# Three V buffers, outer taps ahead of quantise1, a last step and a seam in a new order, and filler matmuls on TensorE

## What is computed

```python
x = x + tanh(g_xattn) * xattn(layernorm(x), ctx, ctx, Wq, Wk, Wv, Wo)   # 16 heads of 16
x = x + tanh(g_ffn)   * ffn(layernorm(x), w1, conv_w, conv_b, w2)
# ffn: h = bit_linear(x, w1)               256 -> 1024
#      h = silu(depthwise_conv1d(h))       3 taps along the tokens of a sequence
#      y = bit_linear(h, w2)               1024 -> 256
# bit_linear: activations rounded to 255 levels by the absolute maximum of their token,
#             weights rounded to -1, 0, 1 by the mean of |w|
```

## Time and profile before

| | |
|---|---|
| median of three runs | 258.53 us (256.13 to 259.03) |
| the profiled execution | 256.48 us, span 253.8 us |
| TensorE matmul busy | 216.5 us (85%) |
| VectorE busy | 189.2 us (75%) |
| ScalarE busy | 162.6 us (64%) |
| POOL busy | 124.8 us (49%) |
| mean granted TensorE clock | 0.959 of 2.4 GHz |

### The profile page before, as it was taken

How to read it: one execution, slowest core, us unless ns; L and a number is a source line. 1 busy time by engine, 2 the same in 40 slices (tenths; PEclk the granted TensorE clock), 3 DMA queues, 4 the chain that set the end, 5 groups by cost and what they waited for, 6 DMA issues and landing times.

```text
span 253.8 us, 6484 instructions
## 1 busy us (share of the span) xinstructions
PE 216.5 (85%) x2384; PEld 175.8 (69%) x2396; DVE 189.2 (75%) x383; ACT 162.6 (64%) x318; POOL 124.8 (49%) x229
## 2 busy tenths in 40 slices
PE   7898989989899899998999989797943799995964
PEld 7786777877768677776777768565633588884853
DVE  3354567879779878888878888777599599996741
ACT  2568785567758787877878768464742477763531
POOL 3320353473455767567675675635367223444440
PEclk9999999999999999999999999978696899998899
DMA  6961011011011010100000000000000011101111
GB/s 177 381 211 41 16 32 43 4 44 41 3 41 33 15 43 3 41 3 21 4 4 0 3 4 0 3 0 3 0 0 0 0 46 41 44 24 42 41 42 62
DMA packets 9489, 9.86 MB, mean 39 GB/s; under 512 B 1011, under 2 KB 9203, under 8 KB 9459
## 3 DMA queue, kind: packets, MB, share of 16 engines
q1 hardware_dynamic: 9458, 9.46, 11.6%
HBM read 7.36 MB, written 2.10 MB: 37 GB/s over the span
## 4 chain that ended last, share of the span: by engine, by line
POOL 31%; issue 23%; DVE 22%; PE 19%; ACT 3%; DMA 1%; POOLq 0%; SPq 0%; DVEq 0%; ACTq 0%
POOL rstd L324 5%; DVE zmax L1088 5%; POOL hid L348 4%; POOL xn L334 4%; DVE y L993 3%; PE ps_av L676 3%; DVE y L996 3%; POOL xn L328 3%; POOL xn L316 3%; POOL rstd L308 3%; POOL var L321 3%; DVE qa L973 3%; PE ps_score L603 2%; PE ps_score L452 2%; DVE xres L1098 2%
## 5 line engine op out<-in xcount | busy, mean ns | idle before, releaser
L937 DVE TENSOR_REDUCE smax<-ps_max 128x8 f32<-128x1024 f32 x31 | 37.9, 1223 | 20.5 <-PE ps_max L462 16.9
L749 ACT ACTIVATE prob<-ps_score 128x1024 f32<-128x1024 f32 x32 | 32.7, 1023 | 18.2 <-PE ps_score L452 17.2
L452 PE MATMUL ps_score<-Qs,KT 32*128 32x128 f32 x512 | 37.8, 286 | 3.5 <-ACT QT L744 1.7
L452 PEld LDWEIGHTS ps_score<-Qs,KT 32*128 32x128 f32 x512 | 32.0, 189 | 11.2 <-issue 10.1
L462 PE MATMUL ps_max<-KT,QT 32*128 32x256 f32 x248 | 35.1, 400 | 0.0
L357 POOL TENSOR_SCALAR zq<-y,zmax 128x1024 f16<-128x1024 f32 x16 | 18.3, 1143 | 30.9 <-issue 14.9
L321 POOL TENSOR_SCALAR var<-mv 128x1 f32<-128x1 f32 x16 | 7.9, 496 | 43.2 <-DVE mv L969 43.1
L423 PE MATMUL ps_proj<-xnT,wq 128*128 128x128 f32 x128 | 18.4, 287 | 6.2 <-ACT xnT L723 6.0
L423 PEld LDWEIGHTS ps_proj<-xnT,wq 128*128 128x128 f32 x128 | 15.6, 191 | 9.1 <-ACT xnT L723 8.7
L462 PEld LDWEIGHTS ps_max<-KT,QT 32*128 32x128 f32 x248 | 21.1, 184 | 0.1
L1088 DVE TENSOR_REDUCE zmax<-y 128x1 f32<-128x1024 f32 x16 | 19.4, 1214 | 2.3 <-ACT y L882 2.3
(11 more groups left out here) (138 smaller groups left out, 537.8 us busy)
## 6 DMA issues: line engine op xcount, KB each, us to landing
cin<-ctxT SPq DMA_DIRECT2D x16, 128.0 KB, 2.1
xres<-x SPq DMA_DIRECT2D x16, 128.0 KB, 2.5
out<-xres SPq DMA_DIRECT2D x16, 128.0 KB, 1.7
w1f<-w1T SPq DMA_DIRECT2D x1, 1024.0 KB, 5.6
w2f<-w2T SPq DMA_DIRECT2D x1, 1024.0 KB, 7.9
wk<-wkT SPq DMA_DIRECT2D x1, 256.0 KB, 2.8
wv<-wvT SPq DMA_DIRECT2D x1, 256.0 KB, 3.9
wq<-wqT SPq DMA_DIRECT2D x1, 256.0 KB, 4.2
```

Source lines behind the costliest of these rows:

```text
L452: mm = pe.matmul(ps_score[:, i * 512 + j * P:i * 512 + (j + 1) * P], KT[b % 3][rows, j * P:(j + 1) * P], Qs[rows, j * P:(j + 1) * P], star ...
L749: act.activation(prob[pair][:, :], ps_score[:, :], ACT.Exp, scale=DH ** -0.5).then_inc(exp_done, 1)
L937: dve.tensor_reduce(dst, first_max(n, pair)[:, :].rearrange("p (g t e k) -> p g t e k", g=PG, t=KD, e=2), AX.X, ALU.max).then_inc(max_done, 1)
```

## The change

V gets a third buffer, so `v_copy(n)` waits for `weigh(n-3)`. In `step` on VectorE the odd tile's outer taps stand ahead of `quantise1`. Step 15 becomes a function `last_step` of its own on three engines, with another order; POOL does its tile before `round1` there. The weight work is spread: a half of a weight sum in each of steps 1 to 4, w1's mean in step 2 and w2's in step 4, w1r's halves in steps 5 and 6. The seam is in a new order on TensorE, ScalarE and VectorE. `y_transpose(12)` and `(13)` move from v = 8 to v = 9, the later two by one as well. `keep_busy` is also put into step 14 and the seam: 4, 3, 2, 3, 12 and 2 matmuls.

```diff
+VB = 3
...
-OPENED.update({LAST - 4: [LAST, LAST + 1], LAST - 3: [LAST + 2], LAST - 2: [LAST + 3]})
+OPENED.update({LAST - 3: [LAST, LAST + 1], LAST - 2: [LAST + 2], LAST - 1: [LAST + 3]})
...
-        V = [sb(f"V{i}", [P, NH * ROW]) for i in range(2)]
+        V = [sb(f"V{i}", [P, NH * ROW]) for i in range(VB)]
...
                 if seq(s - 2):
                     norm2(s - 2)
-                    round1(s - 2)
+                    if s < NB - 1:
+                        round1(s - 2)
                 for T in TILES.get(s, ()):
                     if on_gp(T):
                         dequantise(T)
+                if s == NB - 1:
+                    round1(s - 2)
                 if seq(s + 2):
...
+            def keep_busy(count, bank):
+
+                for i in range(count):
+                    pe.matmul(bank[:, 0:P], ident[:, :], ident[:, :], start=True, stop=True)
...
-                                       V[a % 2][:, h * ROW:(h + 1) * ROW],
+                                       V[a % VB][:, h * ROW:(h + 1) * ROW],
...
                 if seq(n + 1):
                     project_k(n + 1)
-                if s == NB - 1:
-                    y_transpose(0)
+                else:
+                    pe.wait_ge(v_done, NB)
+                    keep_busy(4, ps_k)
+                row_stage(b, 1)
+
+            def last_step():
+                b, a, d = NB - 1, NB - 2, NB - 3
+                T, U_ = TILES[b]
+                project_out(d)
+                hidden(T, LAST)
+                weigh(a)
+                max_transpose(b)
+                int_transpose(d - 1, T)
+                unweighted_transpose(a)
+                row_stage(b, 0)
+                y_transpose(0)
+                hidden(U_, LAST)
+                att_transpose(a)
                 row_stage(b, 1)
...
-            def weight_means():
+            def weight_mean(i):
                 pe.wait_ge(gate_done, 1)
-                pe.wait_ge(abs_done, 1)
+                pe.wait_ge(abs_done[i], 2)
+                if i == 1:
+                    pe.wait_ge(xq_done, 2 * 2)
                 for half in range(2):
-                    mm = pe.matmul(ps_setup[:, 2:4], ones[:, :], abs_sum[:, 2 * half:2 * half + 2],
+                    mm = pe.matmul(ps_setup[:, 2 + i:3 + i], ones[:, :], abs_sum[:, 2 * half + i:2 * half + i + 1],
                                    start=(half == 0), stop=(half == 1))
                 mm.then_inc(sums_ready, 1)
-            step(2, weight_means)
+            step(2, lambda: weight_mean(0))
             pe.wait_ge(mean_done, 1)
             pe.wait_ge(ident16_done, 1)
-            for s in range(3, SB + 2):
+            step(3)
+            step(4, lambda: weight_mean(1))
+            pe.wait_ge(mean_done, 2)
+            step(5)
+            pe.wait_ge(w1q_done, PIECES)
+            for s in range(SB + 2, NB - 1):
                 step(s)
-            pe.wait_ge(w1q_done, PIECES)
-            for s in range(SB + 2, NB):
-                step(s)
+            last_step()
...
             project_out(NB - 2)
             int_transpose(NB - 3, 20)
             weigh(NB - 1)
-            hidden(20, NB - 2)
+            hidden(20, LAST)
             y_transpose(1)
             unweighted_transpose(NB - 1)
-            hidden(21, NB - 2)
+            y_transpose(2)
+            hidden(21, LAST)
+            pe.wait_ge(x1_done, NB - 1)
+            keep_busy(3, ps_xT)
             att_transpose(NB - 1)
-            y_transpose(2)
+            pe.wait_ge(att_done, NB)
+            keep_busy(2, ps_av)
             project_out(NB - 1)
-            hidden(22, NB - 2)
+            keep_busy(3, ps_av)
+            hidden(22, LAST)
+            y_transpose(3)
             int_transpose(NB - 2, 23)
+            keep_busy(12, ps_av)
+            hidden(23, LAST)
             zq_transpose(0)
-            y_transpose(3)
-            hidden(23, NB - 2)
+            keep_busy(2, ps_av)
+            project_down(0)
             int_transpose(NB - 1, 24)
             for v in range(NB):
-                project_down(v)
+                if v > 0:
+                    project_down(v)
                 if v + 1 < NB:
                     zq_transpose(v + 1)
...
-                wait(act, av_ready, NG * (n - 1))
-                act.activation(V[n % 2][:, :].rearrange("p (h w) -> p h w", w=ROW)[:, :, 0:DH],
+                wait(act, av_ready, NG * (n - VB + 1))
+                act.activation(V[n % VB][:, :].rearrange("p (h w) -> p h w", w=ROW)[:, :, 0:DH],
...
                 if seq(a):
                     exponent(a, 1)
-                extra(0)
+                extra()
                 for T in last:
                     middle_tap(T)
...
                 if seq(d - 1):
                     int_copy(d - 1)
-                extra(1)
                 if seq(n):
                     q_copy(n)
...
-                if s == NB - 1:
-                    middle_tap(18)
+            def last_step():
+                b, a, d = NB - 1, NB - 2, NB - 3
+                before, now = TILES[b - 1], TILES[b]
+                exponent(a, 1)
+                middle_tap(before[0])
+                raw_copy(now[0])
+                u_copy(a)
+                middle_tap(before[1])
+                int_copy(d - 1)
+                exponent(b, 0)
+                middle_tap(now[0])
+                att_copy(a)
+                exponent(b, 1)
...
-            def weight_sums(i):
+            def weight_sum(i, k):
                 w, loaded_w = ((w1f, w1_in), (w2f, w2_in))[i]
 
-                def half(k):
+                def half():
                     act.wait_ge(loaded_w, 16)
-                    ac = act.activation(y[:, (2 * i + k) * HID:(2 * i + k + 1) * HID], w[:, k * HID:(k + 1) * HID], ACT.Abs,
-                                        accum_out=abs_sum[:, 2 * k + i:2 * k + i + 1])
-                    if i == 1 and k == 1:
-                        ac.then_inc(abs_done, 1)
+                    act.activation(y[:, (2 * i + k) * HID:(2 * i + k + 1) * HID], w[:, k * HID:(k + 1) * HID], ACT.Abs,
+                                   accum_out=abs_sum[:, 2 * k + i:2 * k + i + 1]).then_inc(abs_done[i], 1)
                 return half
 
-            step(1, weight_sums(0))
+            def first_weights(k):
+                def half():
+                    act.wait_ge(w1q_done, PIECES)
+                    act.activation(w1r[:, k * HID:(k + 1) * HID], w1q[:, k * HID:(k + 1) * HID],
+                                   ACT.Copy).then_inc(w1r_done, 1)
+                return half
+
+            step(1, weight_sum(0, 0))
             act.wait_ge(gate_ready, 1)
             act.activation(gate[:, :], ps_setup[:, 0:2], ACT.Tanh).then_inc(gate_done, 1)
-            step(2, weight_sums(1))
+            step(2, weight_sum(0, 1))
             act.wait_ge(mean_done, 1)
-
-            def first_weights(k):
-                act.wait_ge(w1q_done, PIECES)
-                act.activation(w1r[:, k * HID:(k + 1) * HID], w1q[:, k * HID:(k + 1) * HID], ACT.Copy).then_inc(w1r_done, 1)
-
-            for s in range(3, SB + 1):
+            step(3, weight_sum(1, 0))
+            step(4, weight_sum(1, 1))
+            step(5, first_weights(0))
+            act.wait_ge(small_in, 16)
+            step(6, first_weights(1))
+            for s in range(SB + 3, NB - 1):
                 step(s)
-            step(SB + 1, first_weights)
-            act.wait_ge(small_in, 16)
-            for s in range(SB + 2, NB):
-                step(s)
+            last_step()
...
-            exponent(NB - 1, 1)
-            middle_tap(19)
 
             act.activation(scratch[:, :], ones[:, 0:1], ACT.Silu)
             act.wait_ge(w2q_done, PIECES)
-            act.wait_ge(w1q_done, PIECES)
             u_copy(NB - 1)
             silu(0)
+            middle_tap(19)
             int_copy(NB - 3)
+            silu(1)
             middle_tap(20)
             att_copy(NB - 1)
-            silu(1)
+            silu(2)
             middle_tap(21)
-            silu(2)
+            int_copy(NB - 2)
+            silu(3)
             middle_tap(22)
-            int_copy(NB - 2)
             quantised_copy(0)
-            silu(3)
+            int_copy(NB - 1)
             middle_tap(23)
-            int_copy(NB - 1)
             for v in range(NB):
...
-                dve.wait_ge(scale_done, 1)
+                dve.wait_ge(scale_done, i + 1)
...
                 extra(0)
                 shift_q(b)
+                for T in last[1:2]:
+                    outer_taps(T)
                 if seq(d):
                     quantise1(d)
-                for T in last[1:2]:
-                    outer_taps(T)
                 if seq(a):
                     normalise(a)
-                if d - 1 >= LAST:
-                    remainder(d - 1)
                 if seq(n):
                     row_max(n, 1)
                 for T in tiles[1:2]:
                     dequantise(T)
                 extra(1)
```

(72 more changed lines are left out.)

28 lines of the change are left out of this document (10 added, 18 removed).

## The result

The changed kernel takes **237.93 us** (median of 4 runs, 237.92 to 238.09) against 257.33 (4 runs, 255.90 to 259.03): ratio 0.9245, interval 0.9174 to 0.9316. The profiled execution took 237.92, its span is 236.0 against 253.8. The 17.8 us between the spans fall into three parts: step 15 starts 8.94 earlier (155.81 against 164.75), token_scale(4) another 4.9 earlier, and the last residual2 another 4.0. The start of step 15 scatters by some 0.5 us between executions of the same steps (155.78 to 156.28 in the eight profiles that have them), most of it present by the start of step 2 (27.67 to 28.10).

What follows compares the result with a forecast made beforehand. No engine was full: hand-overs with two TensorE holes bound the step, clock drops and VectorE the rest. Gains 8.6 + 6.2 + 3.2 = 18.0 us take 256.48 to 238.5, plus 0.5: 239.0 us, range 234 to 247.

Steps and rivals of the forecast that it cites:

- The steps: Steps 1 to 14 together gain 8.6 us, with the tile steps 8 to 13 going from 10.70 to 10.0.
- the xnT hole: TensorE's 0.50 us wait for xnT in a step; the third V buffer gains 0.47 us wherever it waits.
- the att hole: TensorE's 0.38 us wait for att in a tile step; att governs and steps 8 to 13 gain 0.70 each.
- The rival that something else sets the steps: POOL's chain or ScalarE's order sets the steps, which gain 0.2 us each; 247 us in all; chance 0.09.
- The port: In the tile steps 0.4 us of POOL time moves free; rival: POOL blocks second tap, 4 us, 243; chance 0.10.
- The seam: Step 15 through token_scale(3) and the hole behind it: gain 6.2 us, with a clock drop at that hole.
- VectorE's walk from token_scale(0) to token_scale(3): On VectorE in the seam: some 16.4 us of work with no waits, so token_scale(3) starts at +29.0.
- Rival B: VectorE waits 3.3 us as before and fillers delay hidden(23); the seam gains 3, not 6.2; 242 us; chance 0.16.
- The entry: Step 15 up to token_scale(0), which was to come at +12.7 us from the step's start, 7.0 earlier.
- Fillers at nothing: Idle matmuls in step 14 and the seam precede TensorE waits, so they were costed at 0.
- rival E: Shifted TensorE holes drop the clock and it stays low, up to 9 us a step; 266 us; chance 0.03.
- The tail: Behind the loop of tiles 24 to 31, project_down(10) starts 3.9 us earlier; 2.4 with a clock drop; 3.2 taken.

Runs made afterwards that it cites:

- the halves: Each tile-step edit alone on the kernel before: third V buffer 254.48 us (ratio 0.9873); odd tile's taps ahead of quantise1 248.05 us (ratio 0.9646).

## Why the prediction was right, and where not

**The steps** (8.6; measured 8.94). By the starts of project_out each step gave: 0.65, 0.73, 0.46, 0.07, 1.07 for steps 1 to 5 (predicted 0.62, 0.75, 0.47, 0.12, 1.07), 0.47 for 6 (0.47), 0.49 for 7 (0.16), 4.32 for 8 to 13 (4.2), 0.68 for 14 (0.7); the rest is rounding. The start of step 2 scatters by 0.4 between executions, so the agreement for step 1 is in part luck. Only step 7 was mis-sized: I counted the xnT hole alone there, at 0.16, and put att at nothing. The runs show that att is most of it: 0.38 with the taps alone, 0.02 with V alone, 0.49 with both. That att governs is shown by the halves: alone, the xnT hole is worth 0.01 a step and the att hole 0.60. The rival that something else sets the steps is out.

**The port.** I moved 0.4 us of POOL time from one pass to the next at no cost to the steps; L330 grew from 0.55 to 0.96, L336 shrank from 0.90 to 0.48, and the step is 9.98. The second tap did stand behind POOL, as the rival said, but for 0.2 us (0.93 against 0.75). This 0.2 lies on the step's chain (tap, quantise1, att, transpose); still it can have cost only about 0.1 us a step, for TensorE's matmul ahead of att's transpose ends at 133.39 and the transpose starts at 133.50. I had also written that no row of before shows a tap held by POOL; one did, shown below. The rows show the order. L330 is issued at 130.62, during the first tap (to 131.15), and ends at 131.58; the second tap is issued at 131.19 and ends at 132.12, 0.54 behind it. In the seam the taps of 170.75, 180.04 and 183.88 end 0.54, 0.53 and 0.53 after POOL's instruction beside them (171.43, 180.49, 184.54). Unblocked, a tap takes 0.73. The Trainium skill (SBUF — State Buffer, Who interferes with whom) says that such instructions exclude each other; the rows agree, save that a held tap ends some 0.53 us behind POOL's instruction, 0.2 less than its 0.73 alone.

**The seam** (6.2; measured 4.9): this is the step that was off, and the term is VectorE's walk from token_scale(0) to token_scale(3). Rival B's waits did not return: VectorE stands nowhere for 0.1 us in it. The entry was right: second row_stage done at +8.7 (8.5), exponent ended at +9.75 (9.7), token_scale(0) at +12.8 (12.7). The walk was laid out at 16.3 us and took 17.49, of which 16.90 busy and 0.59 not. Both parts were to be seen before:
- The 0.59 are gaps of a few hundredths between its 34 instructions. Of the 3.28 us that VectorE didn't work in the earlier trace rows, two waits make 1.54 + 1.22 = 2.76; the other 0.52 were such gaps. I called all 3.28 waits and let them go.
- The 0.5 of work are taps held by POOL: 0.49 + 0.25 + 0.46 = 1.2 in three of them, where the walk had carried over 0.73 from one. That one stands in the kernel before, a tap of 1.48 us beside POOL's quantisation, inside my 14.24 us. I had read the port in the step's rows alone, and didn't ask how many such meetings the new order would have. VectorE's timeline of before, then POOL's:

```profile
192.72 1.48 DVE L996 SCALAR_TENSOR_TENSOR y<-hid,conv,y 128x508 f32<-128x508 f32 x1
```

```profile
192.23 1.45 POOL L357 TENSOR_SCALAR zq<-y,zmax 128x1024 f16<-128x1024 f32 x1
```

The entry's 7.0 us are counted against a profile of the kernel before with two drops in that stretch. With the taps alone, in the old order and without a drop, 3.6 of them were had already. I took the full clock of step 15 for granted; why it came is open.

The last piece, the hole ahead of zq_transpose(1), was taken at 2.9 us with a drop, 0.35 + 1.7 = 2.05; it was 3.32 us, and 2.04 were lost, of which filling it gave back 1.6.

**Fillers at nothing:** right as a cost. For step 14 I also read the earlier trace rows as if the 0.79 us hole and the one before it made the drop in step 15, and rival E rests on that. Without the fillers the 0.79 us hole was back and the drop was not; with three V buffers alone both holes were there (0.82 and 0.79), with 2.19 us of matmuls in 3.80, and the drop was not. The kernel before had 0.76 and 0.79 and 2.20 in 3.75, and 0.53 behind them. What makes the difference is open.

**The tail** (3.2; measured 4.0 by the spans and 4.0 by the run with the old order). project_down(10) starts 4.06 earlier against the loop (5.29 behind token_scale(11), before 9.35), where I had 3.9. I halved the difference for a drop that didn't come: the hole of 1.73 us left the clock at 1.00. The 4.0 is measured against profiles that had the drop in the old tail.

**The sum** came out at 17.8 for 18.0 because a seam 1.3 too high stood against steps and a tail 0.3 and 0.8 too low. That they cancel so well is luck. The 0.5 for the median was not needed: 0.8 us went from outside the span (2.68 to 1.92), which no row explains.

## What to carry to other kernels

Two holes of one engine in one loop don't add. Ask which input governs behind the first; here 0.50 us of one were worth 0.01 alone and 0.12 with the other gone, so the pair has to be judged together. Idle matmuls belong in a hole whose drop delays a hand-over that others wait for, and that is read in the trace after the change, not in the one before. Of two holes of 3.3 us here, filling one was worth next to nothing and filling the other 1.2 us. When work is packed on VectorE, lay POOL's instructions beside it and charge each meeting of a two-input pass with the rest of POOL's instruction (here less 0.2 us).
